# Statistics of the next chunk taken behind the normalisation instead of between its steps, in the last four of 64 chunks

## What is computed

```python
def _gn(v, G=32, eps=1e-5):
    B_, C_, H_, W_ = v.shape
    g = v.reshape(B_, G, C_ // G, H_, W_)
    m = jnp.mean(g, axis=(2, 3, 4), keepdims=True)
    s = jnp.var(g, axis=(2, 3, 4), keepdims=True)
    return ((g - m) / jnp.sqrt(s + eps)).reshape(v.shape)
...
        xp = jnp.pad(x, ((0, 0), (0, 0), (1, 1), (1, 1)))
        xp = xp.at[:, :, DST_R, DST_C].set(xp[:, :, SRC_R, SRC_C])
        up = _conv(xp, w_up * jnp.asarray(_UP), b_up)
        left = _conv(xp, w_left * jnp.asarray(_LEFT), b_left)
        right = _conv(xp, w_right * jnp.asarray(_RIGHT), b_right)
...
        out = out.at[:, :, 0::2, 0::2].set(up)
        out = out.at[:, :, 1::2, 0::2].set(left)
        out = out.at[:, :, 1::2, 1::2].set(right)
        return out * jnp.asarray(OUT_MASK)
...
    x = x + _L0_conv_ref(_gn(x), ...)
```

## Time and profile before

| | us |
|---|---|
| median of three runs | 741.6 (741.59 to 742.24) |
| the profiled execution | 742.11 |
| its span, first to last instruction | 740.3 |
| TensorE matmul busy | 655.8 (89%) |
| VectorE busy | 613.8 (83%) |
| ScalarE busy | 574.8 (78%) |
| GpSimd busy | 473.9 (64%) |
| moved by DMA | 269.62 MB, mean 364 GB/s |
| mean granted TensorE clock | 0.990 of full speed |

### The profile page before, as it was taken

How to read it: one execution, slowest core, us unless ns; L and a number is a source line. 1 busy time by engine, 2 the same in 40 slices (tenths; PEclk the granted TensorE clock), 3 DMA queues, 4 the chain that set the end, 5 groups by cost and what they waited for, 6 DMA issues and landing times.

```text
span 740.3 us, 36046 instructions
## 1 busy us (share of the span) xinstructions
PE 655.8 (89%) x15484; PEld 602.8 (81%) x15484; DVE 613.8 (83%) x1793; ACT 574.8 (78%) x1235; POOL 473.9 (64%) x1109
## 2 busy tenths in 40 slices
PE   1699999999999989889889898898898988989893
PEld 1589999999999888778788787787887878878883
DVE  4999999999999778788787787887977878878740
ACT  3488888988888787787877877878778778787782
POOL 1177777787776765756657657566576575665774
PEclk9989999999999999999999999999999999999997
DMA  8999999999999999999999999999999999999998
GB/s 262 349 362 384 384 380 373 367 367 374 374 356 366 366 367 370 365 379 368 366 369 367 374 370 367 374 365 362 379 361 375 362 366 376 365 365 374 378 352 286
DMA packets 267034, 269.62 MB, mean 364 GB/s; under 512 B 4656, under 2 KB 266800, under 8 KB 266992
## 3 DMA queue, kind: packets, MB, share of 16 engines
q1 hardware_dynamic: 266512, 269.24, 106.0%
q10 hardware_dynamic: 480, 0.00, 0.0%
HBM read 135.01 MB, written 134.22 MB: 364 GB/s over the span
## 4 chain that ended last, share of the span: by engine, by line
DMA 36%; DVE 31%; ACT 12%; POOL 10%; SPq 4%; issue 3%; PE 3%; POOLq 0%; ACTq 0%
DMA xs<-in_x 35%; DVE stats L229 17%; ACT tn L313 12%; DVE tn L277 7%; POOL xs L401 5%; POOL tn L411 4%; SPq L193 3%; PE bank L459 3%; DVE small L261 2%; DMA out<-xs 1%; DVE nmr L272 1%; DVE small L265 1%; DVE rstd L268 1%; DVE var L250 1%; DVE mate L237 0%
## 5 line engine op out<-in xcount | busy, mean ns | idle before, releaser
L459 PE MATMUL bank<-tn,wts 64*64 64x192 f32 (+1 forms) x15360 | 646.9, 325 | 0.0
L459 PEld LDWEIGHTS bank<-tn,wts 64*64 64x64 f32 x15360 | 593.4, 137 | 34.1
L229 DVE BATCH_NORM_STATS2 stats<-xs 128x6 f32<-128x512 f32 x512 | 350.4, 697 | 95.1 <-DMA xs<-in_x 95.1
L401 POOL TENSOR_TENSOR xs<-res,xs 128x192 f32<-128x192 f32 (+6 forms) x775 | 376.1, 530 | 7.7 <-ACT res L336 5.8
L313 ACT ACTIVATE tn<-xs,nmr,rstd 128x256 f32<-128x256 f32 x511 | 258.9, 592 | 78.7 <-DVE nmr L272 78.1
L336 ACT ACTIVATE res<-bank,bias 64x512 f32<-64x512 f32 (+5 forms) x640 | 302.1, 472 | 21.1 <-PE bank L459 10.9
L411 POOL COPY tn<-tn 128x128 f32<-128x128 f32 (+2 forms) x320 | 97.3, 362 | 242.2 <-ACT tn L313 242.2
L277 DVE TENSOR_SCALAR tn<-xs,rstd,nmr 128x256 f32<-128x256 f32 x513 | 181.5, 427 | 2.3
L470 PEld LDWEIGHTS bank<-blank 128*128 128x128 f16 x64 | 6.1, 96 | 82.5 <-ACT res L336 65.8
L470 PE MATMUL bank<-blank 128*128 128x2 f16 x64 | 11.2, 176 | 63.9 <-POOL tn L411 63.8
L307 ACT ACTIVATE std<-var 128x16 f32<-128x16 f32 x64 | 13.8, 216 | 49.7 <-DVE var L250 49.7
(11 more groups left out here) (18 smaller groups left out, 24.1 us busy)
## 6 DMA issues: line engine op xcount, KB each, us to landing
out<-xs SPq DMA_DIRECT2D x128, 1024.0 KB, 11.1
xs<-in_x SPq DMA_DIRECT2D x126, 1024.0 KB, 11.1
xs<-in_x SPq DMA_DIRECT2D x4, 512.0 KB, 8.4
tn<-in_L_conv_w_up SPq DMA_DIRECT2D x1, 256.0 KB, 3.8
tn<-in_L_conv_w_left SPq DMA_DIRECT2D x1, 256.0 KB, 4.3
tn<-in_L_conv_w_right SPq DMA_DIRECT2D x1, 256.0 KB, 6.2
bias<-in_L_conv_b_up ACTq DMA_DIRECT2D x2, 0.2 KB, 4.5
bias<-in_L_conv_b_left ACTq DMA_DIRECT2D x2, 0.2 KB, 6.0
```

The costliest lines, as they stand in the source:

```text
L229: last = nc.vector.bn_stats(stats[:, k % 2, 2 * u:2 * u + 2].rearrange("p g a -> p (g a)"), both)
L401: last = nc.gpsimd.tensor_tensor(onto, frm, onto, ALU.add)
L459: last = nc.tensor.matmul(psum[bank + j][to:to + C, at:at + cols], wts[first:first + C, NT * rect[0] + n, :], taps(b, rect, tap, first), s ...
```

## The change

In chunks 60 to 63 VectorE's small steps run with no statistics between them. Chunks 61, 62 and 63 get their statistics when the chunk before has been normalised, in two calls of four instructions each, so that each half still waits for its own load. Up to chunk 59 all is as it was; chunk 63 had nothing between its steps before either.

```diff
+TAIL = 4
...
             for k in range(1, NCHUNK):
-                moments(k, k + 1)
-                norms(k, k + 1)
+                ahead = k + 1 if k < NCHUNK - TAIL else NCHUNK
+                moments(k, ahead)
+                norms(k, ahead)
                 normalise(k)
                 if k + 1 < NCHUNK:
+                    if ahead == NCHUNK:
+                        bn(k + 1, 0, G // 4)
+                        bn(k + 1, G // 4, G // 2)
                     dve.wait_ge(bn_done, k + 2)
```

## The result

The changed kernel takes 743.56 us (median of nine runs, 742.93 to 745.14) against 741.58 for the kernel before in the same comparison (nine runs, 740.70 to 742.24). The ratio is 1.0033, with a 95% interval of 1.0023 to 1.0043: slower by a third of a per cent, 2.0 us by the medians. The forecast was 743.3, its range 740.6 to 745.0.

The account below looks back on a forecast made before the run. Loads bound the loop, then a fixed tail ran to the end. Freed normalising would collide with GpSimd's additions, starting TensorE's chunk 63 1.7 us later: 743.8 us from the profiled 742.11, 743.3 against the median; range 740.6 to 745.0.

Parts of the forecast that it names:

- What bounds the loop: Late chunks: loads bound it at 11.4 us a chunk; a statistics instruction between small steps waits 1.87 us.
- The collision: Chunks 60 to 62: VectorE's normalising falls into GpSimd's additions; in chunk 60 the eight take 4.98 instead of 2.68 us.
- the number of turns charged to the small steps: Waits of small steps for GpSimd's additions from chunk 61: one charged at 0.45 us, bounds none and two (plus 0.75).
- The sum: TensorE's start of chunk 63: 1.4 us later with one turn, 2.0 with two, 0.6 with none; 1.7 taken.
- The sign: Whole kernel's time: chance 0.51 above 743.1 us, 0.37 within measuring accuracy, 0.11 and a little below 740.1.
- rival three: Chunks 60 to 62: each addition also waits for each normalising instruction, 1.6 us a chunk, 748.2 us; chance 0.04.
- Rival one: Late chunks: normalising and additions fall beside each other, VectorE's period is 9.85 us, time 739.5 us; chance 0.11.
- Rival two: Late chunks: the collision is lighter than in chunk 63, periods near 11.5 us, 741 to 742.5 us; chance 0.16.
- The period of 11.5: VectorE's late chunks: the us per chunk below which TensorE would start chunk 63 earlier than before.
- The check list: Signs in the late trace: eight normalising instructions 4.2 to 5 us, durations near 0.7, TensorE's chunk 63 wait some 1.5.

Follow-up runs that it names:

- the held-back additions: The changed kernel, with GpSimd's additions in the last four chunks waiting until VectorE has normalised: 740.4 us, ratio 0.9990; the same over eight chunks 739.7 us, ratio 0.9975.
- the split order: The changed kernel, with only the last four statistics instructions behind the normalisation and the first four left between the steps of moments: 741.36 us, ratio 1.0001.
- the changed kernel with TAIL = 8: The changed kernel with the new order in four more late chunks (TAIL 8 instead of 4): 747.41 us, ratio 1.0077 against the kernel before.

## Why the prediction was right

**What bounds the loop** held: it was the load between the small steps, and with it gone VectorE waited for no load behind 663.93. Its own length bounds it now, and ScalarE's root waits 3.25 to 3.40 us for var.

**The collision** held for chunk 60 to a hundredth (2.97 and 4.98), and the price by whole turns behind GpSimd's additions held for the others. The term that was mis-sized, inside its bounds, is the number of turns charged to the small steps. I charged one and gave two as the bound. Both rstd and nmr wait, in each of chunks 61, 62 and 63, so it is two: the eight end 5.65 behind the additions' start (690.15 - 684.50) where I had 5.37, with 5.67 as the bound. The period is 12.33 instead of 12.2. That the two engines alternate was read rightly, if loosely: in the trace of before, chunk 63's first two normalising instructions each end 0.14 us behind an addition (708.82 behind 708.68, 709.45 behind 709.31), not with it.

**The sum** for the delay of TensorE's start of chunk 63 was 1.4 later with one turn, 2.0 with two, 1.7 taken; 1.81 was measured. That two turns came to 1.8 and not to 2.0 has for the most part a small reason of its own: the additions start 0.72 behind the evacuation (684.50 - 683.78), not 0.87 as in the earlier trace rows, where GpSimd was still at its wraps. That makes 0.15 in each of chunks 61 and 62.

**The sign was nearer to the edge than it had to be.** I gave "slower" 0.51 (two thirds of 0.68 and rival three make 0.49). With the two turns counted the forecast would have been 743.6. The trace of before had what was needed: in chunk 63 L268 took 0.32 and L265 0.28, both held up by mere wraps, which are shorter than the additions. And in chunk 60 a small step stood beside the additions (673.65 to 679.44) and took three times as long as alone:

```profile
676.71 0.58 DVE L261 SCALAR_TENSOR_TENSOR small<-var,small 128x16 f32<-128x16 f32 x1
```

That the forecast came within 0.3 us owes something to luck: it took 1.7, between one turn and two, and the two turns would have made 2.0 had the additions not started earlier than read.

**The rivals.** Rival one, VectorE running free, is what the held-back additions come near to, and it is faster there, by 0.10% with four chunks and 0.25% with eight; not by the 2.1 us I gave it, since the additions then fall on `moments` and the period is 11.05, not 9.85. Rival two, a lighter collision, is what the split order makes of it: 11.7 us a chunk and no change. The period of 11.5, up to which TensorE was to start chunk 63 no later than before, was a little too strict. Rival three, full exclusion on both sides, is out: the additions took 6.25 and not 8.4. VectorE's instruction does wait for an addition's end, but GpSimd loses only some 0.05 us per turn. (Its own price was a little low: eight turns of 0.22 are 1.8 us a chunk, not 1.6.) By the rule of the Trainium skill (SBUF — State Buffer, Who interferes with whom) either side blocks fully; the runs show that for VectorE alone.

**The check list** held but for two lines. Durations near 0.7 us were measured in chunk 60 only (median 0.71); from chunk 61 on the median is 0.58, since most of the eight meet the later, shorter additions. And TensorE's wait in front of chunk 63 was to be 1.5 us and was 0.90. The clock hid the rest: chunk 62's convolution took 11.34 us instead of 10.05, without which the wait would have been 2.2. In it the granted clock's mean was 0.58 from 708 to 710 and 0.57 from 710 to 712, so it fell from 2.4 to 1.2 GHz for some 3.4 us of these four. It cost nothing, for the wraps came later still.

## What to carry to other kernels

When a wait is taken out, ask which engine was idle beside the stalled one and which was working: the work set free may land on another engine's instructions and be held up by them. A wait can be a useful spacer. Price a moved block of work from the one place in the trace where it already stands in its new company (here the last chunk), not from where it stands alone. And a pace read late in a run need not be its pace early: look at several stretches before a change is spread over the whole loop.

## What the runs showed of the hardware

- VectorE's normalising of 128 x 256 float32 elements, SBUF to SBUF, takes a new instruction every 0.32 us alone and one every 0.64 us beside the first of GpSimd's twelve additions ((4.98 - 0.49) / 7), 0.53 beside the later ones ((4.16 - 0.43) / 7). With 15 instead of 16 rows it takes one every 0.43 us beside the additions, and the additions take what they take alone.
- Whether its factors are constants or read per partition made no difference to the collision in chunks 61 to 63 (4.15 against 4.16 us for eight); in chunk 60 the constants took 4.59 against 4.98.
- Statistics instructions, with one input, took 0.68 to 0.72 us, beside the additions as elsewhere; steps of 128 x 16 with two inputs took up to 0.76 instead of 0.17.
- TensorE's granted clock fell to half for some 3.4 us after it had waited 1.19, then 2.15 us in front of two successive chunks; in the kernel before, with waits of 1.0 to 1.6 us, it stayed at 1.00 through this stretch. The length of one wait alone does not decide: in the changed kernel with TAIL = 8 a convolution behind a wait of 2.43 us ran at 1.00 (10.05 us), and the next, behind 1.90, did not (11.33). What decides was not tried.
